# Moving six bank-marking matmuls of a recurrence into earlier gaps of TensorE, and adding eight filler matmuls before a small averaging product

## What is computed

```python
    def _L1_ffn_ref(x, W, V, gamma, beta):
        Wx = jnp.einsum('bti,hi->bth', x, W)
        flat = Wx.reshape(B * T, H)
        mean = jnp.mean(flat, axis=0)
        var = jnp.var(flat, axis=0)
        Wx = ((flat - mean) * jax.lax.rsqrt(var + BN_EPS) * gamma + beta).reshape(B, T, H)
        Vt = V.T

        def step(yt, wx_t):
            yt = jax.nn.sigmoid(wx_t + yt @ Vt)
            return (yt, yt)
        y0 = jnp.zeros((B, H), dtype=Wx.dtype)
        _, ys = jax.lax.scan(step, y0, jnp.swapaxes(Wx, 0, 1))
        return jnp.swapaxes(ys, 0, 1)
```

## Time and profile before

| | us |
|---|---|
| median of 3 runs | 230.27 |
| the runs | 228.68, 230.27, 230.61 |
| the profiled execution | 229.49 |
| its span | 227.7 |
| mean share of full TensorE clock | 0.965 |

### The profile page before, as it was taken

How to read it: one execution, slowest core, us unless ns; L and a number is a source line. 1 busy time by engine, 2 the same in 40 slices (tenths; PEclk the granted TensorE clock), 3 DMA queues, 4 the chain that set the end, 5 groups by cost and what they waited for, 6 DMA issues and landing times. The chain is left out here.

```text
span 227.7 us, 3379 instructions
## 1 busy us (share of the span) xinstructions
PE 196.7 (86%) x1150; PEld 96.0 (42%) x1150; DVE 161.2 (71%) x294; ACT 169.7 (75%) x307; POOL 28.7 (13%) x44
## 2 busy tenths in 40 slices
PE   0686999999999797979699999999999998599960
PEld 0562646545555443413234343434343423266640
DVE  0327819999999763894958497877777795576980
ACT  4028299789779698996988999999999974365640
POOL 6000000091060053080101010101010000000000
PEclk9997999999999999979999999999999999889995
DMA  6940020089799349199631607080800000000016
GB/s 188 370 135 3 3 72 1 1 227 296 194 259 340 100 146 304 42 353 252 173 79 40 179 10 212 0 219 0 219 3 0 3 0 0 0 3 3 0 50 241
DMA packets 26885, 26.87 MB, mean 118 GB/s; under 512 B 1550, under 2 KB 25806, under 8 KB 26740
## 3 DMA queue, kind: packets, MB, share of 16 engines
q1 hardware_dynamic: 26868, 26.64, 39.9%
HBM read 14.74 MB, written 11.88 MB: 117 GB/s over the span
## 5 line engine op out<-in xcount | busy, mean ns | idle before, releaser
L510 ACT ACTIVATE arena<-ps 128x800 f32<-128x800 f32 (+1 forms) x56 | 44.5, 797 | 6.9 <-PE ps L1053 4.6
L517 ACT ACTIVATE arena<-arena 128x800 f32<-128x800 f32 (+1 forms) x56 | 46.4, 831 | 0.0
L1053 PE MATMUL ps<-qa,ka 128*128 128x400 bf16 (+1 forms) x128 | 35.4, 340 | 3.6 <-ACT arena L510 2.0
L1053 PE MATMUL ps<-qb,kb 96*128 96x400 bf16 (+1 forms) x128 | 35.4, 339 | 0.0
L742 DVE TENSOR_TENSOR psum<-arena 128x400 f32<-128x400 f32 x32 | 19.6, 612 | 13.8 <-ACT arena L517 13.8
L742 DVE TENSOR_TENSOR psum<-psum,arena 128x400 f32<-128x400 f32 x32 | 19.5, 610 | 7.5 <-ACT arena L517 6.2
L1053 PEld LDWEIGHTS ps<-qa,ka 128*128 128x128 bf16 (+1 forms) x128 | 10.4, 97 | 27.6 <-ACT arena L510 12.5
L1086 PE MATMUL ps<-arena,vb 128*32 128x400 f32 x192 | 21.6, 525 | 0.2 <-issue 0.2
L751 DVE RECIPROCAL arena<-ps 128x400 f32<-128x400 f32 x7 | 18.6, 2650 | 0.0
L664 DVE COPY arena<-arena 32x400 f32<-32x400 f32 x48 | 17.2, 358 | 0.9
L587 ACT ACTIVATE yb<-ps 128x160 f32<-128x160 f32 x36 | 11.0, 305 | 8.0 <-PE ps L1170 6.7
(11 more groups left out here) (146 smaller groups left out, 354.3 us busy)
## 6 DMA issues: line engine op xcount, KB each, us to landing
dka<-arena SPq DMA_DIRECT2D x16, 200.0 KB, 3.1
dqa<-arena SPq DMA_DIRECT2D x16, 200.0 KB, 3.2
ka<-dka SPq DMA_DIRECT2D x8, 400.0 KB
qa<-dqa SPq DMA_DIRECT2D x8, 400.0 KB
arena<-x_tok SPq DMA_DIRECT2D x4, 400.0 KB
t<-x SPq DMA_DIRECT2D x1, 1600.0 KB, 11.7
dkb<-arena SPq DMA_DIRECT2D x8, 200.0 KB, 3.5
dqb<-arena SPq DMA_DIRECT2D x8, 200.0 KB, 3.7
```

The costliest lines, as they stand in the source:

```text
L510: nc.scalar.activation(prob[par][:, lo:hi, :], ps[:, o:o + hi - lo, 0:N], ACT.Exp, scale=2.0).then_inc(e1_done, 1)
L517: nc.scalar.activation(p, p, ACT.Exp).then_inc(p_ready, 1)
L1053: last = mm_(ps[row:row + keys, bank, 0:N], kk[par][0:rows, b, o:o + keys], qq[par][0:rows, b, :], start=first, stop=not first, skip_group ...
```

## The change

Banks: group 7 uses (3, 7) in place of (2, 3), so bank 2 is free early. `FILL_BANK` and `SMALL_BANK` are exchanged (7 and 3). The primes go in the order 4, 5, 6, 0, 1, 2. Banks 4 and 5 are primed between `center2` and `variance2` of group 7; banks 6, 0, 1, 2 behind its `project2`, which has one more wait (`u2_ready`, so that bank 1 has been read). Then come eight new fills into bank `PRIME_ORDER[2]`, which is 6, then the averaging product, and behind it 18 fills in place of six primes and ten fills. The fill of a step writes bank 7.

```diff
-FILLS_FIRST = 10
+FILLS_STATS = 8
+FILLS_FIRST = 18
-        PRIME_ORDER = (0, 4, 1, 5, 2, 6)
-        FILL_BANK, SMALL_BANK = 3, 7
+        PRIME_ORDER = (4, 5, 6, 0, 1, 2)
+        FILL_BANK, SMALL_BANK = 7, 3
-        LAST_BANKS = {G - 2: (0, 1), G - 1: (2, 3)}
+        LAST_BANKS = {G - 2: (0, 1), G - 1: (3, 7)}
...
-            def fill():
-
-                mm_(ps[:, FILL_BANK, 0:FILL], ka[0][:, 0, 0:P], ka[0][:, 0, 0:FILL], start=True, stop=True)
-
+            def fill(bank=FILL_BANK):
+
+                mm_(ps[:, bank, 0:FILL], ka[0][:, 0, 0:P], ka[0][:, 0, 0:FILL], start=True, stop=True)
+
+            center2(G - 1, LAST_BANKS[G - 1])
+            for bank in PRIME_ORDER[:2]:
+                prime(bank)
+            variance2(G - 1, LAST_BANKS[G - 1])
+            pe.wait_ge(u2_ready, G - 1)
+            project2(G - 1, LAST_BANKS[G - 1])
+            for bank in PRIME_ORDER[2:]:
+                prime(bank)
+            for _ in range(FILLS_STATS):
+                fill(PRIME_ORDER[2])
             pe.wait_ge(bn_c, 2)
             mm_(ps[:, SMALL_BANK, 0:2], c_("avg4"), mv, start=True, stop=True).then_inc(bn_pe, 1)
-            for bank in PRIME_ORDER:
-                prime(bank)
             for _ in range(FILLS_FIRST):
                 fill()
```

More of the change, by code:

```diff
@@ L1148, in _ @@
             project2(G - 2, LAST_BANKS[G - 2])
-            center2(G - 1, LAST_BANKS[G - 1])
-            variance2(G - 1, LAST_BANKS[G - 1])
-            project2(G - 1, LAST_BANKS[G - 1])
             def prime(bank):
```

## The result

| | before | after |
|---|---|---|
| median of 4 runs, us | 230.44 | 768.66 |
| the runs, us | 228.68 to 231.43 | 763.99 to 772.23 |
| the profiled execution, us | 229.49 | 770.25 |
| its span, us | 227.7 | 768.5 |
| mean share of full TensorE clock | 0.965 | 0.901 |

The change makes the kernel slower, by a ratio of 3.3344, 95% interval [3.3186, 3.3503].

The account below looks back on a forecast made before the run. It took the wait chain with primes and fills at half clock to bound the kernel. Flag 221.65, entry 2, 39 sweeps 534.3, sum 7.0, store 7.4 and 1.8 outside the span gave 774.2, with the median 775; range 715 to 880.

Parts of the forecast that it names:

- The part that decides: Eight fills behind bank 6's prime unmark columns 256 to 479; the comparison fails and 39 sweeps of 13.7 us run.
- reading by the bank: A matmul with start=True clears the marks of its whole bank, then marks its own columns; given 0.86.
- entering the loop: Between the flag and the loop's first sweep, not shown in the trace: 0 to 5 us, taken as 2.
- last state of half 0 to first step of half 1: In each loop sweep, VectorE's copies and seeds ahead of half 1, with two hand-overs: 3.7 us.
- falls of the clock, mean of a sweep: TensorE idling in each loop sweep lowers its clock: up to 1.1 us a sweep or nothing, taken as 0.6.
- waits and jumps, a sweep: Waits against registers and the loop's jump back: between nothing and 2 us a sweep, taken as 0.1.
- one sweep: One pass of the loop of 39 sweeps: 13.7 us, with bounds 12.6 and 16.1.
- second sum and store: After the loop, the output is summed once more, 7.0 us, and stored, 7.4 us.
- The part that was meant: Before the recurrence, moved primes and new fills let its first step start earlier: worth 0.2 to 0.9 us, taken as 0.85.
- Marks by the column: Rival: a start marks only the columns it writes, bank 6 stays marked, the gain arrives: 229.4 us, chance 0.09.
- the clock falls all the same: Rival: marks by the column, but TensorE's clock still falls around the averaging product or first steps: 230.1 to 230.5, chance 0.04.
- the comparison passes: Rival: marks cleared by the bank, but overwritten states agree by sigmoid saturation: 229.4 us with wrong values, chance 0.01.

Follow-up runs that it names:

- 480 columns: Changed kernel with four fills of 480 columns in place of eight of 256, still behind bank 6's prime with a start: 230.8 us, ratio 0.997.
- `start=False`: Changed kernel with its eight fills of 256 columns at the same place but without a start: 229.95 us, ratio 0.996.
- two unused columns: Kernel with the fills before the primes, plus one start=True matmul behind the primes over columns 510 and 511 of bank 6: 767.17 us.
- 320-column run: Kernel with the fills before the primes, plus one start=True matmul behind the primes over columns 0 to 319 of bank 6: 769.69 us.
- run with fills in the loop: Changed kernel with ten more fills behind the first step of half 0 in each sweep of the loop: 726.3 us.
- seeds in the other order: Changed kernel with VectorE's loop seeds reordered, the first seed of each half before the second ones: 673.03 us.
- without the eighteen fills: Kernel with the eight fills before the primes, minus the eighteen fills behind the averaging product: ratio to before 1.0047.
- without the eight fills: Kernel with the fills put before the primes, minus the eight fills before the averaging product: ratio to before 0.9957.

## Why the prediction was right

**The part that decides.** The step was that the eight fills clear marks of bank 6 outside their columns, that the comparison fails and that the loop runs. The runs with 480 columns, with `start=False` and with two unused columns show each half of it. That places 7 and 8 both do harm was argued; the 320-column run shows that a wrong place 8 is enough, and no run isolates place 7.

The chance of 0.86 rested on the code, a two-column product with a bank of its own, and that argument was weaker than I took it for. In the kernel before the averaging product stands ahead of the primes (197.44, primes from 197.69), so under either reading it can unmark nothing that they mark; only the product of the comparison stands behind them. A bank of its own can also have other reasons, since VectorE reads the result at 197.87, while TensorE is already writing the primed banks. That the reading by the bank came true is no evidence for this argument, and in that part there was luck.

**The sum.** Step by step, predicted and measured in the profiled execution:

| term | predicted | measured |
|---|---|---|
| flag written, behind the centring | 30.16 | 30.23 |
| entering the loop | 2 | 1.8 |
| last state of half 0 to first step of half 1 | 3.7 | 3.18 |
| to step 1 of half 0 | 0.4 | 0.48 |
| eight periods | 8.0 | 7.97 |
| last step to its state | 0.86 | 0.81 |
| falls of the clock, mean of a sweep | 0.6 | 1.16 |
| waits and jumps, a sweep | 0.1 | 0 seen |
| one sweep | 13.7 | 13.60 |
| second sum and store | 14.4 | 12.4 |

(The four rows from the last state to the last state are those of the undisturbed sweep.) The sweep came out right because two sizes were off in opposite ways, and that is luck. The seeds were priced at 0.73 each and the copy at 0.31, from pairs of which the last end was counted as well; in a row the seeds start 0.68 apart, and the first seed follows the copy after 0.16. The clock cost about twice what I took: 1.16 us, the difference of the mean sweep and the undisturbed one. The price of a fall was sized well, 1.1 us predicted and 1.2 measured in most sweeps (13.64 against 12.44). What I had wrong was how often it comes: 0.6 is half of that price, as if every second sweep were spared, and 38 of 39 had it. They had it although TensorE's two idle stretches were shorter than I had worked out, 0.72 and 1.47 us where I had 1.2 and 1.9. The run with fills in the loop confirms the size: 42 us over 39 sweeps are 1.1 a sweep. Nothing is left for waits against registers or jumps: 3.18 + 0.48 + 7.97 + 0.81 is 12.44. Of the 2.0 us that the end was priced too high, 0.9 are the second sum and 1.1 the store. The nine additions follow each other in 5.76 us, 0.64 each, where I had taken their isolated 0.73; from the issue of the store (762.25) to the end are 6.25 us, where I had taken the 7.4 of the kernel before. Why this store was shorter was not looked into.

**The part that was meant.** The primes in the first gap, the new wait and the order behind the projection cost nothing: the averaging product starts 5.96 us behind the centring, before 5.95. Eighteen fills took 2.1 us with the modelled end of the last one, predicted 2.0. The gain was 0.84 us at the first step (predicted 0.87) and 0.78 at the flag. One cover was thinner than I said: the first two primes are over by 194.26 in the modelled ends, 0.19 us before the variance matmul starts.

**The rivals.** Marks by the column fell with the two-column run. That the clock falls all the same fell in the trace of after, which shows 1.00 through both idle stretches, of 1.13 and 1.01 us. That the comparison passes fell with the flag.

## What to carry to other kernels

Where a kernel adds to data that another engine wrote into PSUM, the marks are not safe because nobody writes their columns. After marking, keep every matmul with `start=True` out of the bank, however few or unused its columns are; only one that covers all the used columns did no harm here. A filler is not without effect because nobody reads it; give it a bank with nothing open, or put it before the marking. And a kernel with a fallback hides such an error as time, so look first at instruction counts: 1632 where 72 were expected said more than any duration.

## What the runs showed of the hardware that I had not expected

The clock can fall on short idle stretches. In the loop TensorE idled 0.72 us, ran one step and a fill, and idled 1.47 us, and in 37 of the 38 sweeps behind the first the granted clock then went to half, for about 3.3 us; ten fills there took nearly all of the falls away (mean clock 0.901 to 0.985). With the seeds in the other order only the 0.72 us were left, and the clock held as well (0.986). Yet before the recurrence it held over idle stretches of 1.13 and 1.01 us with 2.4 us of work between them. The prediction had longer stretches and gave the fall only half of its price.

The fall can also come after the idle time is over: without the eighteen fills TensorE had been at work again for 0.84 us when the clock fell, and without the eight fills for 1.2 us. The price is then paid by the steps and not by the filler: these took 0.74 in place of 0.51 us each, and with two to a period the recurrence ended 1.1 us later.
